# A linear-attention block rebuilt: joint query and key products, swapped halves, one reciprocal for two tiles

## The chip, the core and the metric

One core of a Trainium2 chip runs one program. TensorE (PE, with PEld for its loads of stationary operands), VectorE (DVE), ScalarE (ACT), GpSimd (POOL) and SyncE (SP, which here only issues transfers and waits) each work through their own list of instructions, and semaphores tie the lists together. The time is that of one execution on the device in microseconds; lower is better.

## What is computed

The input is 2 images of 512 channels and 32 x 32 pixels, in float32. Four layers follow each other: an attention with sampled keys and a position bias that a small network computes, a deformable convolution with a gate, a linear attention, and a multi-head attention. The change is in the third:

```python
def delu(x):
    return PARAM * jax.nn.relu(x) + jnp.exp(PARAM * jnp.minimum(x, 0.0))
xf = x.reshape(B, C, N)
Q = jnp.einsum('dc,bcn->bdn', wq, xf) + bq[None, :, None]
K = jnp.einsum('dc,bcn->bdn', wk, xf) + bk[None, :, None]
V = jnp.einsum('ec,bcn->ben', wv, xf) + bv[None, :, None]
Qf = delu(Q).transpose(0, 2, 1)
Kf = delu(K)
KV = jnp.einsum('bmn,bcn->bmc', Kf, V)
norm = 1.0 / jnp.einsum('bnd,bd->bn', Qf, jnp.sum(Kf, axis=-1) + EPS)
attn = jnp.einsum('bnd,bdc,bn->bcn', Qf, KV, norm)
return x + gamma[0] * attn.reshape(B, C, H, W)
```

B is 2, C is 512, N is 1024 pixels of an image, queries and keys have d = 64 rows and PARAM is 10.

## The kernel before

`layer2` (lines 1624 to 1858) is one block of the program: all engines enter it together and leave it together, and the next block's work begins when the last of them is done. The tile X holds the activations of both images in SBUF, 128 partitions by 4 channel groups (k) by 2048 pixels. The pixels are cut into four tiles of 512 (n; tiles 0 and 1 are image b = 0, tiles 2 and 3 image b = 1), and an image into 8 pieces of 128 pixels (c). Everything is float32.

Ahead, SP loads the query, key and value weights and the bias rows of keys and values, all counted on one semaphore `w_in`, and then the weights of the next layer (`g["prefetch"]`). TensorE, ScalarE and VectorE all wait for the five loads together.

For each image TensorE then does the following, written out at lines 1749 to 1761:

- `keys` (L1696): for each piece of 128 pixels four products, with the pixels as the stationary operand and 64 columns of key weights streamed past. So keys come out with pixels on the partitions.
- `queries` (L1687): for a tile of 512 pixels four products with 64 columns of query weights as the stationary operand. Queries come out with their 64 rows on 64 partitions.
- `pixels` (L1705): 32 transposes of X, four for each piece, in two PSUM buffers which ScalarE (L1796) and VectorE (L1838) empty in turn.
- `key_products` (L1717, L1719): keys times pixels, 8 products of 512 columns, and the sums of the keys, 8 products of one column.
- `key_values` (L1725, L1729): that result is copied, turned and multiplied by the value weights.
- `outputs` (L1738, L1746): for each tile the norms, and then four products for the four channel groups, in two PSUM buffers that VectorE adds to X (L1822).

The value weights are applied after keys and pixels have been multiplied, so values are never computed for each pixel. The features (`delu`) are made from a minimum (VectorE), an Exp (ScalarE), a maximum times ten (VectorE for keys, GpSimd for queries at L1769) and an addition (VectorE). The outputs of the first image stand behind the second image's queries, and ahead of its key products. VectorE makes the norms' reciprocals one tile after the other (L1814), each followed by a scaling of the queries (L1817):

```python
for n in range(2 * b, 2 * b + 2):
    v.wait_ge(n_mm, n + 1)
    v.reciprocal(RN[:, n, :], norms[n % 2]).then_inc(rn_ready, 1)
    v.wait_ge(rn_ready, n + 1)
    v.wait_ge(q_ready, n + 1)
    v.tensor_tensor(QN[:, n, :], QR[:, n, :], RN[:, n, :], ALU.mult).then_inc(qn_ready, 1)
```

In passing the block splits the next layer's weights into twelve rounded pieces and their remainders: ScalarE rounds (L1807), GpSimd subtracts (L1773). The block after this one begins with statistics of X on VectorE (L1969).

In the profile the tiles of this block have names with `lin_` in front, X is `net_x`.

## Time and profile before

| | |
|---|---|
| time, median of 3 runs | 4188.23 us (4186.56 to 4192.63) |
| the profiled execution's own time | 4190.17 us |
| its span | 4188.4 us |
| TensorE's mean granted clock | 0.957 of full speed |
| busy, TensorE products | 3866.5 us (92%) |
| busy, VectorE | 2981.1 us (71%) |
| busy, ScalarE | 2591.7 us (62%) |
| busy, GpSimd | 2088.0 us (50%) |

Start times in the rows below are microseconds from the start of the span. A float32 product of TensorE has two rows in the profile, each with half of the passes; a transpose has one. So "x8" is four products or eight transposes.
### The profile page before, as it was taken

Reading aid. Unit: us, or ns where it says so; the run is one execution under the profiler, and the core shown is the slowest. Engines: PE = TensorE matmul, PEld = TensorE weight load, DVE = VectorE, ACT = ScalarE, POOL = GpSimd, SP = SyncE. Lnnn points to the kernel's source line nnn. Section 1 sums busy time; section 2 is a strip of 40 time slices with the busy share of each in tenths; the row PEclk is TensorE's granted clock in tenths of the full one; section 3 lists DMA queues with packets and bytes.
Section 4 is the critical chain, followed back from the end, with each engine's and each line's share of the span. In section 5 each row is a group of like instructions: output and inputs, shape, how many; then the busy total and the mean of one; then the engine's idle time right before and its main releaser. Section 6 shows DMA issues by size and latency. Waiting matters only on the chain. (4 is left out here: it accounts for less than half of the span.)

```text
span 4188.4 us, 67038 instructions
## 1 busy us (share of the span) xinstructions
PE 3866.5 (92%) x18696; PEld 2423.2 (58%) x18696; DVE 2981.1 (71%) x4504; ACT 2591.7 (62%) x4616; POOL 2088.0 (50%) x1870
## 2 busy tenths in 40 slices
PE   6899999999999999999998999989888467969999
PEld 3555555555555555555556788837667343835553
DVE  7888888888888888888887433376999936245552
ACT  5899999999999999999996433232221431213331
POOL 0555555555555555555552455415777620036663
PEclk8999999999999999999999999999999777979999
DMA  1200000000000000000002000028999911453312
GB/s 49 103 9 12 9 10 9 9 9 9 12 9 10 9 9 9 9 12 9 10 9 87 28 5 1 0 82 340 394 390 397 377 64 62 174 116 71 72 41 81
DMA packets 150518, 326.82 MB, mean 78 GB/s; under 512 B 45785, under 2 KB 50073, under 8 KB 149517
## 3 DMA queue, kind: packets, MB, share of 16 engines
q1 hardware_dynamic: 108940, 174.46, 13.5%
q0 software_dynamic: 41472, 151.01, 9.0%
q8 instruction: 59, 0.97, 0.1%
q14 instruction: 47, 0.38, 0.0%
HBM read 246.14 MB, written 79.04 MB: 78 GB/s over the span
## 5 line engine op out<-in xcount | busy, mean ns | idle before, releaser
L558 POOL TENSOR_TENSOR cpb_sum<-cpb_tab 128x512 f32<-128x512 f32 x1028 | 1046.7, 1051 | 965.0 <-DVE cpb_r L688 964.7
L669 ACT ACTIVATE cpb_h<-cpb_z,net_vec 128x512 f32<-128x512 f32 x1536 | 1007.8, 699 | 50.5 <-PE cpb_z L609 37.8
L606 PE MATMUL cpb_z<-cpb_r,cpb_w2a 128*128 128x512 f32 x2048 | 858.1, 419 | 22.9 <-DVE cpb_h L729 22.9
L688 DVE SCALAR_TENSOR_TENSOR cpb_r<-cpb_sum,cpb_r 128x512 fp32r<-128x512 f32 x1024 | 696.7, 711 | 187.9 <-ACT cpb_r L663 187.9
L607 PE MATMUL cpb_z<-cpb_r,cpb_w2b 128*128 128x512 f32 x2048 | 802.3, 392 | 0.0
L609 PE MATMUL cpb_z<-cpb_r,cpb_w2a 128*128 128x512 f32 x2048 | 800.2, 391 | 0.0
L688 DVE SCALAR_TENSOR_TENSOR cpb_r<-cpb_z,cpb_r 128x512 fp32r<-128x512 f32 x1028 | 662.0, 686 | 160.0 <-ACT cpb_r L663 154.6
L663 ACT ACTIVATE cpb_r<-cpb_z 128x512 fp32r<-128x512 f32 x1028 | 561.1, 604 | 126.6 <-PE cpb_z L593 126.6
L663 ACT ACTIVATE cpb_r<-cpb_sum 128x512 fp32r<-128x512 f32 x1024 | 598.0, 648 | 2.0 <-POOL cpb_sum L558 2.0
L606 PEld LDWEIGHTS cpb_z<-cpb_r,cpb_w2a 128*128 128x128 f32 x2048 | 383.8, 187 | 366.1 <-issue 300.4
L618 PE MATMUL cpb_zo<-cpb_h,cpb_w3w 128*32 128x512 f32 x3584 | 477.3, 605 | 0.0
L1569 DVE SCALAR_TENSOR_TENSOR dc_acc<-dc_g,dc_wt,dc_acc 128x512 f32<-128x512 f32 x560 | 443.3, 801 | 34.9 <-DMA dc_g<-conv_out,dc_idx 19.2
L609 PEld LDWEIGHTS cpb_z<-cpb_r,cpb_w2a 128*128 128x128 f32 x2048 | 384.9, 188 | 87.4
L607 PEld LDWEIGHTS cpb_z<-cpb_r,cpb_w2b 128*128 128x128 f32 x2048 | 385.7, 188 | 63.7
L1260 POOL DMA_INDIRECT dc_g<-conv_out,dc_idx x288 | 322.9, 1121 | 169.2 <-DVE dc_acc L1569 84.8
L729 DVE TENSOR_SCALAR cpb_h<-cpb_z,net_vec 128x512 f32<-128x512 f32 x512 | 380.4, 743 | 0.0
L1442 ACT COPY dc_ys<-dc_py 128x512 f32<-128x512 f32 x144 | 84.6, 588 | 364.3 <-DMA conv_out<-dc_ys 219.2
L2262 ACT ACTIVATE net_x<-sa_pb 128x512 f32<-128x512 f32 x256 | 139.2, 595 | 267.5 <-PE sa_pb L2188 267.5
L1042 POOL TENSOR_TENSOR mlp_wb<-l_w,mlp_wa 128x512 fp32r<-128x512 f32 x128 | 196.8, 1557 | 173.5 <-ACT mlp_wa L1006 173.5
L2158 POOL TENSOR_TENSOR sa_acc<-sa_acc,net_x 128x512 f32<-128x512 f32 x192 | 240.9, 1279 | 71.5 <-ACT net_x L2262 70.6
L1326 PE MATMUL dc_py<-net_conv_w,dc_dh 128*128 128x512 f32 x576 | 234.1, 406 | 45.3 <-ACT dc_ys L1442 41.3
L2277 DVE TENSOR_REDUCE sa_mxp<-sa_pa 128x1 f32<-128x512 f32 x224 | 144.4, 686 | 147.5 <-PE sa_pa L2172 147.5
(358 smaller groups left out, 5326.5 us busy)
## 6 DMA issues: line engine op xcount, KB each, us to landing
conv_out<-dc_ys SPq DMA_DIRECT2D x576, 64.0 KB, 6.1
cpb_log<-log_dram SPq DMA_DIRECT2D x66, 256.0 KB, 3.2
qk_parts<-gn_r SPq DMA_DIRECT2D x64, 256.0 KB, 2.0
dc_wr<-in_dc_wT SPq DMA_DIRECT2D x9, 1024.0 KB, 5.9
bias_dram<-cpb_bst SPq DMA_DIRECT2D x520, 8.0 KB
net_x<-in_x SPq DMA_DIRECT2D x8, 1024.0 KB, 11.1
sa_qa<-qk_parts SPq DMA_DIRECT2D x16, 512.0 KB
sa_ka<-qk_parts SPq DMA_DIRECT2D x16, 512.0 KB
```

The source lines that it names most:

```text
L558: pool.tensor_tensor(SUM[:, r, :].rearrange("p (y x) -> p y x", x=W), TAB[:, slot, r, 0, :].unsqueeze(1).broadcast_to([P, NF // W, W]), TA ...
L606: pe.matmul(z2[:, bank, :], W2A[:], R1[:, k, :], start=True, stop=False)
L607: pe.matmul(z2[:, bank, :], W2B[:], R1[:, k, :], start=False, stop=False)
L609: pe.matmul(z2[:, bank, :], W2A[:], R2[:, k, :], start=False, stop=True).then_inc(z2_ready, 1)
L618: mm = pe.matmul(zo[32 * r:32 * r + 32, :], W3W[:, half * 4 + c, :], H2[:, (quad * 4 + r) % 8, :], start=(quad == 0), stop=False)
L663: act.activation(R1[:, t % RING, :], first_layer(t), ACT.Relu).then_inc(r1_ready, 1)
L669: act.activation(H2[:, t % 8, :], z2[:, t % 3, :], ACT.Relu, bias=V("cpb_b2")).then_inc(h2a, 1)
L688: v.scalar_tensor_tensor(R2[:, t % RING, :], first_layer(t), 0.0, R1[:, t % RING, :].bitcast(F32), ALU.max, ALU.subtract).then_inc(r2_read ...
L729: v.tensor_scalar(H2[:, (t + 2) % 8, :], z2[:, (t + 2) % 3, :], V("cpb_b2"), 0.0, ALU.add, ALU.max).then_inc(h2v, 1)
L1260: pool.indirect_dma_start(out=G[:, u % GR, y, :], out_offset=None, in_=table[tap % SLOTS][b], in_offset=bass.IndirectOffsetOnAxis(ap=IDX[: ...
L1569: v.scalar_tensor_tensor(o, G[:, u % GR, k // 2, (k % 2) * C:(k % 2 + 1) * C], WT[:, k, col:col + 1], DCB[:] if tap == 0 and k == 0 else o ...
L2158: pool.tensor_tensor(acc, ET[:, 0, u, :] if k == 1 else acc, ET[:, k, u, :], ALU.add).then_inc(added, 1)
```

## The change

The change is inside the linear attention, and in how its weights are laid out in memory. What it does:

- One weight tile `WQK` holds, for each channel group, two stationary operands of 128 columns: queries then keys for even tiles of 512 pixels, keys then queries for odd tiles. `queries_keys(n)` makes both with four products. In even tiles queries are on partitions 0 to 63 and keys on 64 to 127, in odd tiles the other way round. The products of pixels with key weights go away.
- The features of a whole tile, queries and keys, are made together: VectorE adds the bias and takes the minimum (`low`), ScalarE takes Relu of the biased product (`high`) and Exp, VectorE multiplies by ten and adds (`feature`). GpSimd has no part in it.
- Keys are turned by TensorE: 4 transposes per tile (`keys`), copied to SBUF by ScalarE, and doubled by a copy on VectorE, so that key products, sums, and all that follows from them stand on 128 partitions, twice the same 64.
- The norms of the two tiles of an image go to the two halves of one PSUM tile, on partitions 0 to 63 and 64 to 127, and VectorE takes one reciprocal of 128 partitions (`inverse`) and then scales the two tiles (`scaled`).
- The outputs read the half of the doubled operand that lies on the partitions of their queries.
- TensorE waits at its start for the joint weights only. Value weights and value biases have a semaphore of their own, waited for ahead of `key_values(0)`.
- The order of all four lists is written out by hand. The second image's keys and key products come before the outputs of the first, of which two come before the second norms and six after the second value product.

```diff
-            sp.dma_start(WQ[:], d["wqT"].rearrange("(k p) o -> p k o", p=P)).then_inc(w_in, 16)
-            sp.dma_start(WK[:], d["wkT"].rearrange("(k p) o -> p k o", p=P)).then_inc(w_in, 16)
+            sp.dma_start(WQK[:], d["wqkT"].rearrange("(k p) a o -> p k a o", p=P)).then_inc(wqk_in, 16)
             sp.dma_start(WV[:], d["wvT"].rearrange("(k p) o -> p k o", p=P)).then_inc(w_in, 16)
-            sp.dma_start(BK[:], d["bk_rows"]).then_inc(w_in, 16)
             sp.dma_start(BV[:], d["bv_rows"]).then_inc(w_in, 16)
...
-            def queries(n):
-                if n:
-                    pe.wait_ge(q_raw, n)
+            def queries_keys(n):
+                if n >= 2:
+                    pe.wait_ge(hi_ready, n - 1)
                 for k in range(CT):
-                    mm = pe.matmul(pq[:], WQ[:, k, :], X[:, k, n * NF:(n + 1) * NF], start=(k == 0), stop=(k == CT - 1))
-                mm.then_inc(q_mm, 1)
-
-            def keys(b):
-                if b:
-                    pe.wait_ge(k_raw, b)
-                for c in range(NC):
-                    at = b * HW + c * P
-                    for k in range(CT):
-                        mm = pe.matmul(pk[:, c, :], X[:, k, at:at + P], WK[:, k, :], start=(k == 0), stop=(k == CT - 1))
-                mm.then_inc(k_mm, 1)
+                    mm = pe.matmul(pq[:, n % 2, :], WQK[:, k, n % 2, :], X[:, k, n * NF:(n + 1) * NF],
+                                   start=(k == 0), stop=(k == CT - 1))
+                mm.then_inc(qk_mm, 1)
...
+            def keys(b):
+                if b:
+                    pe.wait_ge(kr_a, 2 * b)
+                    pe.wait_ge(ks_ready, b)
+                for n in range(2 * b, 2 * b + 2):
+                    pe.wait_ge(f_ready, n + 1)
+                    for c in range(NC // 2):
+                        mm = pe.transpose(pk[:, n % 2, c, :], F[:, n, c * P:(c + 1) * P], ident[:])
+                mm.then_inc(k_mm, 1)
+
...
                     pe.wait_ge(kv_ready, b)
-                    pe.wait_ge(ks_ready, b)
                 for c in range(NC):
-                    pe.matmul(pkx[:], KR[:, b, c, :], XT[:, b, c, :], start=(c == 0), stop=(c == NC - 1))
+                    pe.matmul(pks, KR[:, c].rearrange("p a d -> p (a d)"), ONE[:], start=(c == 0), stop=(c == NC - 1))
                 for c in range(NC):
-                    mm = pe.matmul(pks[:, 0:1], KR[:, b, c, :], ONE[:], start=(c == 0), stop=(c == NC - 1))
+                    mm = pe.matmul(pkx[:], KR[:, c].rearrange("p a d -> p (a d)"), XT[:, b, c, :],
+                                   start=(c == 0), stop=(c == NC - 1))
                 mm.then_inc(kx_mm, 1)
...
-            def outputs(b):
+            def norms(b):
                 pe.wait_ge(ksb_ready, b + 1)
+                if b:
+                    pe.wait_ge(rn_ready, b)
                 for n in range(2 * b, 2 * b + 2):
-                    pe.wait_ge(q_ready, n + 1)
-                    if n >= 2:
-                        pe.wait_ge(rn_ready, n - 1)
-                    pe.matmul(norms[n % 2], KSB[:, b, :], QR[:, n, :], start=True, stop=True).then_inc(n_mm, 1)
+                    rows = of_queries(n)
+                    mm = pe.matmul(pn[rows, :], KSB[rows, b, :], F[rows, n, :], start=True, stop=True)
+                mm.then_inc(n_mm, 1)
...
-            pe.wait_ge(w_in, 80)
+            pe.wait_ge(wqk_in, 16)
+            queries_keys(0)
+            queries_keys(1)
+            pixels(0)
+            queries_keys(2)
+            keys(0)
+            queries_keys(3)
             pe.wait_ge(one, 1)
-            for b in range(B):
-                keys(b)
-                queries(2 * b)
-                pixels(b)
-                queries(2 * b + 1)
-                if b:
-                    pe.wait_ge(q_raw, 2 * b + 2)
-                    outputs(b - 1)
-                key_products(b)
-                key_values(b)
-            outputs(B - 1)
+            key_products(0)
+            pixels(1)
+            pe.wait_ge(w_in, 32)
+            key_values(0)
+            norms(0)
+            keys(1)
+            key_products(1)
+            outputs(0, 0, 2)
+            norms(1)
+            key_values(1)
+            outputs(0, 2, 2 * CT)
+            outputs(1, 0, 2 * CT)
...
-            for n in range(NT):
-                pool.wait_ge(q_raw, n + 1)
-                pool.tensor_scalar(QR[:, n, :], QT[:, n, :], 0.0, PARAM, ALU.max, ALU.mult).then_inc(q_high, 1)
-                if n == 1:
-                    for i, (whole, high, low) in enumerate(PIECES):
...
+            high(0)
+            exponential(0)
+            high(1)
+            pixels(0, 0)
+            exponential(1)
+            for c in range(2, NC, 2):
+                pixels(0, c)
+            high(2)
+            keys(0)
+            exponential(2)
+            high(3)
+            exponential(3)
+            act.wait_ge(weights_in, 64)
+            for i, (whole, part, _) in enumerate(PIECES):
+                act.copy(part, whole).then_inc(split_h, 1)
+            for c in range(0, NC, 2):
+                pixels(1, c)
+            key_products(0)
+            keys(1)
+            key_products(1)
...
+            def low(n):
+                v.wait_ge(qk_mm, n + 1)
+                v.tensor_scalar(LO[:, n, :], pq[:, n % 2, :], V("bqk", n % 2), 0.0, ALU.add, ALU.min).then_inc(lo_min, 1)
+
+            def feature(n):
+                v.wait_ge(hi_ready, n + 1)
+                v.wait_ge(lo_exp, n + 1)
+                v.scalar_tensor_tensor(F[:, n, :], HI[:, n, :], PARAM, LO[:, n, :], ALU.mult, ALU.add).then_inc(f_ready, 1)
...
+            def keys(b):
+                v.wait_ge(kr_a, 2 * b + 2)
+                v.tensor_copy(KR[:, :, 1, :], KR[:, :, 0, :]).then_inc(kr_v, 1)
...
+            def inverse(b):
+                v.wait_ge(n_mm, b + 1)
+                if b:
+                    v.wait_ge(qn_ready, 2 * b)
+                v.reciprocal(RN[:], pn[:]).then_inc(rn_ready, 1)
+
+            def scaled(n):
+                rows = of_queries(n)
+                v.wait_ge(rn_ready, n // 2 + 1)
+                v.tensor_tensor(QN[rows, n // 2, :], F[rows, n, :], RN[rows, :], ALU.mult).then_inc(qn_ready, 1)
...
+            low(0)
+            low(1)
+            feature(0)
+            pixels(0, 1)
+            feature(1)
+            for c in range(3, NC, 2):
+                pixels(0, c)
+            low(2)
+            keys(0)
+            feature(2)
+            low(3)
+            feature(3)
+            key_sums(0)
+            for c in range(1, NC, 2):
+                pixels(1, c)
+            v.wait_ge(w_in, 32)
+            key_values(0)
+            inverse(0)
+            keys(1)
+            scaled(0)
+            scaled(1)
+            key_sums(1)
+            output(0)
+            output(1)
+            inverse(1)
+            scaled(2)
+            scaled(3)
+            key_values(1)
+            for i in range(2, NT * CT):
+                output(i)
...
-            "wqT": i["L2_wq"].T, "wkT": i["L2_wk"].T, "wvT": i["L2_wv"].T,
-            "bk_rows": every(i["L2_bk"]), "bv_rows": every(i["L2_bv"])[0:DH],
+            "wqkT": np.stack([np.concatenate([i["L2_wq"], i["L2_wk"]]).T, np.concatenate([i["L2_wk"], i["L2_wq"]]).T], axis=1),
+            "wvT": i["L2_wv"].T, "bv_rows": every(i["L2_bv"]),```

TensorE's list of the block, first its beginning to the first value product, before. `pk` holds keys, `pq` queries, `px` what is transposed, `pkx` key products and values, `pks` the sums:

```order
L1696 MATMUL lin_pk<-lin_wk,net_x 128x64 x32
L1687 MATMUL lin_pq<-net_x,lin_wq 64x512 x4
L1705 MATMUL lin_px<-net_ident,net_x 128x128 x32
L1687 MATMUL lin_pq<-net_x,lin_wq 64x512 x4
L1717 MATMUL lin_pkx<-lin_xt,lin_kr 64x512 x8
L1719 MATMUL lin_pks<-lin_one,lin_kr 64x1 x8
L1725 MATMUL lin_px<-net_ident,lin_kx 128x64 x4
L1729 MATMUL lin_pkx<-lin_wv,lin_kxt 64x512 x4
```

And the same place on TensorE in the changed program, where `pk` holds the turned keys and the sums:

```order
L1688 MATMUL lin_pq<-net_x,lin_wqk 128x512 x8
L1698 MATMUL lin_px<-net_ident,net_x 128x128 x32
L1688 MATMUL lin_pq<-net_x,lin_wqk 128x512 x4
L1709 MATMUL lin_pk<-net_ident,lin_f 128x128 x8
L1688 MATMUL lin_pq<-net_x,lin_wqk 128x512 x4
L1719 MATMUL lin_pk<-lin_one,lin_kr 128x1 x8
L1721 MATMUL lin_pkx<-lin_xt,lin_kr 128x512 x8
L1698 MATMUL lin_px<-net_ident,net_x 128x128 x32
L1732 MATMUL lin_px<-net_ident,lin_kx 128x128 x4
L1736 MATMUL lin_pkx<-lin_wv,lin_kxt 128x512 x4
```

The 32 products of 64 columns ahead of the first queries are gone; the queries and keys of both images and the second image's transposes have moved ahead of the first value product.

TensorE's list from the first norms to the end of the block, before (`pq` and `pk` take the norms, `pa` the outputs):

```order
L1738 MATMUL lin_pq<-lin_qr,lin_ksb 64x512
L1738 MATMUL lin_pk<-lin_qr,lin_ksb 64x512
L1746 MATMUL lin_pa<-lin_qm,lin_kv 128x512 x8
L1717 MATMUL lin_pkx<-lin_xt,lin_kr 64x512 x8
L1719 MATMUL lin_pks<-lin_one,lin_kr 64x1 x8
L1725 MATMUL lin_px<-net_ident,lin_kx 128x64 x4
L1729 MATMUL lin_pkx<-lin_wv,lin_kxt 64x512 x4
L1738 MATMUL lin_pq<-lin_qr,lin_ksb 64x512
L1738 MATMUL lin_pk<-lin_qr,lin_ksb 64x512
L1746 MATMUL lin_pa<-lin_qm,lin_kv 128x512 x8
```

And in the changed program, where `pn` takes the norms of both tiles and `pq` the outputs:

```order
L1745 MATMUL lin_pn<-lin_f,lin_ksb 64x512 x2
L1709 MATMUL lin_pk<-net_ident,lin_f 128x128 x8
L1719 MATMUL lin_pk<-lin_one,lin_kr 128x1 x8
L1721 MATMUL lin_pkx<-lin_xt,lin_kr 128x512 x8
L1756 MATMUL lin_pq<-lin_qn,lin_kv 128x512 x2
L1745 MATMUL lin_pn<-lin_f,lin_ksb 64x512 x2
L1732 MATMUL lin_px<-net_ident,lin_kx 128x128 x4
L1736 MATMUL lin_pkx<-lin_wv,lin_kxt 128x512 x4
L1756 MATMUL lin_pq<-lin_qn,lin_kv 128x512 x14
```

The outputs of the first image have moved behind the key products of the second, and 14 of 16 now stand in one row at the end.

VectorE's list in the changed program, from the first value result to the second:

```order
L1865 SCALAR_TENSOR_TENSOR lin_kv<-lin_bv,lin_ks,lin_pkx 128x512
L1871 RECIPROCAL lin_rn<-lin_pn 128x512
L1855 COPY lin_kr<-lin_kr 128x8x64
L1876 TENSOR_TENSOR lin_qn<-lin_f,lin_rn 64x512 x2
L1859 COPY lin_ks<-lin_pk 128x1
L1861 TENSOR_SCALAR lin_ksb<-lin_ks 128x64
L1882 SCALAR_TENSOR_TENSOR net_x<-lin_pq,net_vec,net_x 128x512 x2
L1871 RECIPROCAL lin_rn<-lin_pn 128x512
L1876 TENSOR_TENSOR lin_qn<-lin_f,lin_rn 64x512 x2
L1865 SCALAR_TENSOR_TENSOR lin_kv<-lin_bv,lin_ks,lin_pkx 128x512
```

Each reciprocal is one of 128 partitions, and the copy that doubles the second image's keys stands behind the first of them.

## Rows read from the trace of the kernel before

**Rows 1.** Timeline of the transfer queue: start us, us, what; its first load.

```profile
3384.45 0.41 SPq L1670 DMA_DIRECT2D lin_wq<-in_wqT  x1
```

**Rows 2.** Timeline of VectorE, the block's last addition.

```profile
3514.01 0.75 DVE L1822 SCALAR_TENSOR_TENSOR net_x<-lin_pa,net_vec,net_x 128x512 f32<-128x512 f32 x1 [0.96 <-PE lin_pa L1746]
```

**Rows 3.** Timeline of TensorE's products: start us, us, what, count, idle time before.

```profile
3393.39 13.92 PE L1696 MATMUL lin_pk<-lin_wk,net_x 128*128 128x64 f32 x64 [13.56 <-DMA lin_bv<-in_bv_rows]
3407.23 5.89 PE L1687 MATMUL lin_pq<-net_x,lin_wq 128*64 128x512 f32 x8
3413.06 1.10 PE L1705 MATMUL lin_px<-net_ident,net_x 128*128 128x128 f32 x8
3414.39 4.08 PE L1705 MATMUL lin_px<-net_ident,net_x 128*128 128x128 f32 x24 [0.24 <-ACT lin_xt L1796]
3418.40 3.65 PE L1687 MATMUL lin_pq<-net_x,lin_wq 128*64 128x512 f32 x8
...
3428.75 1.04 PE L1719 MATMUL lin_pks<-lin_one,lin_kr 128*64 128x1 f32 x16
3430.46 0.46 PE L1725 MATMUL lin_px<-net_ident,lin_kx 64*128 64x64 f32 x4 [0.67 <-ACT lin_kx L1799]
3431.38 5.34 PE L1729 MATMUL lin_pkx<-lin_wv,lin_kxt 128*64 128x512 f32 x8 [0.46 <-ACT lin_kxt L1801]
3436.66 7.36 PE L1696 MATMUL lin_pk<-lin_wk,net_x 128*128 128x64 f32 x64
...
3457.29 1.07 PE L1738 MATMUL lin_pq<-lin_qr,lin_ksb 64*64 64x512 f32 x2 [0.77 <-ACT lin_qt L1783]
3458.20 1.02 PE L1738 MATMUL lin_pk<-lin_qr,lin_ksb 64*64 64x512 f32 x2
3462.61 3.75 PE L1746 MATMUL lin_pa<-lin_qm,lin_kv 64*128 64x512 f32 x4 [3.39 <-DVE lin_qm L1817]
3467.16 10.60 PE L1746 MATMUL lin_pa<-lin_qm,lin_kv 64*128 64x512 f32 x12 [0.81 <-DVE net_x L1822]
...
3488.39 3.65 PE L1729 MATMUL lin_pkx<-lin_wv,lin_kxt 128*64 128x512 f32 x8 [0.46 <-ACT lin_kxt L1801]
```

**Rows 4.** Busy us by stretch: PE, PEld, DVE, ACT, POOL; then PEclk, DMA share, GB/s.

```profile
3411.00:3414.00 3.00, 3.00 (x12) 1.23 (x10) 0.00 (x0) 0.84 (x2) 0.07 (x1) 0.87 0.00 0
...
3417.00:3420.00 3.00, 2.87 (x13) 1.44 (x13) 1.71 (x3) 0.59 (x2) 0.00 (x0) 1.00 0.00 0
...
3432.00:3435.00 3.00, 3.00 (x6) 0.81 (x4) 0.00 (x0) 3.00 (x7) 2.04 (x2) 0.54 0.01 3
...
3441.00:3444.00 3.00, 3.00 (x28) 2.93 (x28) 0.00 (x0) 0.00 (x0) 3.00 (x4) 1.00 0.00 0
...
3459.00:3462.00 3.00, 0.21 (x1) 0.00 (x0) 2.96 (x2) 0.00 (x0) 0.46 (x1) 0.60 0.00 0
...
3474.00:3477.00 3.00, 3.00 (x5) 0.95 (x3) 1.50 (x2) 0.00 (x0) 0.00 (x0) 0.50 0.00 0
```

**Rows 5.** Loads of the block: queue, operation, count, KB, median us from issue to landing.

```profile
l3o_w_qk<-in_w_qkT SPq DMA_DIRECT2D x1, 2048.0 KB, 12.4
lin_wv<-in_wvT SPq DMA_DIRECT2D x1, 1024.0 KB, 5.5
...
lin_wq<-in_wqT SPq DMA_DIRECT2D x1, 128.0 KB, 2.4
```

**Rows 6.** Groups of instructions by form, block alone: busy us, mean ns, idle before.

```profile
L1822 DVE SCALAR_TENSOR_TENSOR net_x<-lin_pa,net_vec,net_x 128x512 f32<-128x512 f32 x16 | 11.8, 746 | 12.6 <-PE lin_pa L1746 12.6
L1773 POOL TENSOR_TENSOR l3w_wq_low<-l3o_w_qk,l3w_wq_high 128x512 fp32r<-128x512 f32 x8 | 11.1, 1420 | 0.0
...
L1814 DVE RECIPROCAL lin_rn<-lin_pq 64x512 f32<-64x512 f32 x2 | 6.7, 3350 | 1.3 <-PE lin_pq L1738 1.3
...
L1779 ACT ACT_TABLE_LOAD x1 | 1.3, 1283 | 27.8 <-DVE lin_km L1831 27.8
...
L1831 DVE TENSOR_SCALAR lin_km<-lin_kt 128x512 f32<-128x512 f32 x2 | 0.9, 438 | 0.1
```

More of the change, by code:

```diff
@@ new lines, in exponential, with pixels @@
+            def exponential(n):
+                act.activation(LO[:, n, :], LO[:, n, :], ACT.Exp, scale=PARAM).then_inc(lo_exp, 1)
+            def pixels(b, c):
+                act.wait_ge(xt_mm, b * NC + c + 1)
+                act.copy(XT[:, b, c, :], px[:, 0, :]).then_inc(xt_a, 1)
+            def keys(b):
+                act.wait_ge(k_mm, b + 1)
+                if b:
+                    act.wait_ge(kx_mm, b)
+                for n in range(2):
+                    act.copy(KR[:, n * NC // 2:(n + 1) * NC // 2, 0, :], pk[:, n, :, of_keys(n)]).then_inc(kr_a, 1)
```

171 lines of the change are left out of this document (65 added, 106 removed).

## The prediction

> **What bounds the kernel now.** The change touches one block of the program, the linear attention. The page's shares are averages over all blocks and say nothing of it, so I read its stretch in the timelines of the queue and of VectorE for the ends, in TensorE's timeline for the order, then in the table of stretches with the granted clock, and last in the lists of loads and of groups by form for prices.
>
> The block begins with its loads at 3384.45 [rows 1] and ends with VectorE's last addition at 3514.01 plus 0.75, so 3514.76 [rows 2]: 130.3 us. TensorE's rows [rows 3], in which every float32 product counts twice and a transpose once, are to be read as one chain: apart from two waits they follow each other almost without a gap, so TensorE bounds the block, and its waits are at the start (13.56 us until the last of five loads, the rows of value biases, has landed) and in the middle (3.39 us until VectorE has finished the reciprocals). The reader is to see three more things in these rows. The 32 key products of 64 columns cost 13.92 us the first time and 7.36 us the second. The outputs cost 10.60 us for six products, 1.71 each once the tail of about 0.3 is taken off, where the query products cost 3.65 for four, 0.91 each. The value product costs 5.34 once and 3.65 the other time. Each of these is a factor of up to two, and the clock column explains all of them [rows 4]: 0.50 is 1.2 GHz and 1.00 is 2.4 GHz. It is 0.50 during the outputs, 1.00 in the second key stage, 0.54 in the stretch of the slow value product. It fell at the reciprocals (0.60 in 3459 to 3462). At the first query product (3407.23) it was low and a mean of 0.87 over 3411 to 3414 puts its rise 0.26 of the way in, at 3411.8, 4.5 us after that product began. The key stage before it had kept TensorE busy for 13.9 us without a rise.
>
> **The change part by part.** I rebuild TensorE's chain, since it orders everything. Durations are those of one profiled execution of 4190.17 us, 1.9 above the median of the runs.
>
> *Start.* TensorE now waits for one load, the joint weights of 512 KB. Nearest rows: 128 KB lands 2.4 us after its issue, 1024 KB behind others after 5.5 [rows 5]. So it lands between 3386.9 and 3390.0; I take 3.1 us, 3387.6, nearer the small one because nothing is queued ahead of it. TensorE starts there instead of at 3393.39: 5.8 us earlier (3.4 to 6.5).
>
> *Queries and keys.* 64 key products in two stages (13.92 + 7.36) and 16 query products of 64 columns become 16 products of 128 columns. The output of 128 columns costs no more time if the cost goes by the 512 streamed columns: 0.91 at 2.4 GHz. The first two groups start at 1.2 GHz: 4.5 us at 1.71 each give 2.6 products, the other 5.4 at 0.91 give 4.9, together **9.4 us**. Groups 2 and 3 are 3.65 each. The keys now have to be turned by 16 transposes, 0.1375 each from 8 in 1.10 [rows 3]: 1.1 per half. Together 3.65 + 1.1 + 3.65 = **8.4**.
>
> *Pixels.* The 32 transposes of a half stay; they are paced by the copies, 0.68 per four (24 in 4.08 [rows 3]), 5.4 per half. In the first half the two copying engines now also make the first features, and ScalarE loads its Exp table (1283 ns [rows 6]) between the first query result and the second. On VectorE the features of tile 1 wait for ScalarE's second Exp ahead of its second copy, which puts the last transposes 0.4 later: **5.8 and 5.4**.
>
> *Key products.* The 8 products of 512 columns per half stay, 8 x 0.91 = 7.3. The sums move ahead of them and their stationary operand is now 128 columns wide: 16 loads of 64 columns took 1.04, 64 loads of 128 columns 7.36, 0.115 each, so 16 take 1.85. **9.15 per half**, twice.
>
> *Values.* First half: wait for ScalarE's copy 0.6, transposes 0.55, wait for the next copy 0.65 (it was 0.46 for a tile half as wide, and 0.67 was the wait for the first copy [rows 3]), product 3.65: **5.45**. Second half: the first copy lies under the norms, so 0.55 + 0.6 + 3.65 = 4.8.
>
> *Norms and reciprocals.* The four norm products stay, 0.9 each, the pitch from 3457.29 to 3458.20 [rows 3]. Per half, two reciprocals of 64 partitions (3350 ns each [rows 6]) become one of 128 partitions; no row has one of 128, and bounds are 3.35, if the 512 elements of a partition set it, and 6.7, if all elements do. I take 3.35, since the operations on 128 partitions beside it have 512 elements too and take 0.44 and 0.75 [rows 6], no more per element of a partition than its own. In the first half it stands ahead of the copy that doubles the keys (0.44 from the nearest operation with one input between SBUF tiles [rows 6]) on VectorE, and the key products of the second half are queued behind that copy: norms **1.8**, then **3.9** until TensorE goes on, under which the 8 transposes of keys (1.1) are hidden. In the second half it is covered by the value product, 0.55 + 0.6 + 3.65 = 4.8 against 3.35 + 1.3 for the two scalings; nothing waits. If that cover went, 3.35 would return.
>
> *Outputs.* Two of the first half's outputs go before the second norms (1.8, and norms 1.8, values 4.8: together **8.4**), and 14 stand at the end. VectorE needs 746 ns for one [rows 6], below TensorE's 0.91; with two buffers I take 0.95 each, **13.3**, if the clock is at 2.4 GHz, and the last addition 0.75.
>
> Sum: 9.4 + 5.8 + 8.4 + 9.15 + 5.4 + 5.45 + 1.8 + 3.9 + 9.15 + 8.4 + 13.3 + 0.75 = 80.9, so the end at 3468.5, 46.3 us earlier.
>
> *The clock gives some back.* The wait of 3.9 follows two 64-row products; in the trace such a wait brought 1.2 GHz (0.60 in 3459 to 3462 [rows 4]). The sums and the first products after it then run slow: the sums at 13.92/64 = 0.2175 a load instead of 0.115, 1.7 more, and some 3.4 us of products at half rate, 1.7 more: 3.4. Before each value product stand transposes and two short waits; there the clock fell in one of two cases, at 5.34 - 3.65 = 1.7: 1.7 for the two. 46.3 - 5.1 = **41.2 us**.
>
> *At nothing.* ScalarE's twelve rounding copies of the next layer's weights now stand ahead of its second set of pixel copies; they end about when the first key products do. GpSimd loses its four feature operations and keeps twelve subtractions at 1420 ns [rows 6], 17 us from about 3414, done before VectorE's next copy between SBUF tiles on the path; if that copy met them it could cost 1 us. SP's loads for the next layer stand behind a first load that is 256 KB bigger; the longest took 12.4 us from its issue [rows 5], and its first use moves to about 3413, 28 us after the block's start. Everything after the block reads what it read before and only starts earlier.
>
> Where the two norm products of a half stand in the array is new: they now use different halves of its rows and of its columns. The rows have products of this shape one behind the other, at a pitch of 0.9 [rows 3], and the sum takes them so; side by side they would cost 0.9 a half less. The Trainium skill, "TensorE: Matmul & The Clock Gate", Part 3 (Packing small matmuls), says that products in different row groups run concurrently; by it the sum would be 79.1 in place of 80.9. No row here shows such a pair, so this stands as rival E.
>
> **The rivals.**
>
> *A, the forecast: the last 14 outputs run at 2.4 GHz.* For it: at the second key stage TensorE's work was light too (short streams between loads), and a clock that was high stayed high (1.00 in 3441 to 3444), though the same stage had not raised a low one; and a pixel stage kept it as well (1.00 in 3417 to 3420) [rows 4]. The outputs come directly behind the value product, not behind an idle wait. 41.2 us off.
>
> *B: the outputs run at 1.2 GHz.* For it: the output stage of the trace did, for 10.6 us of unbroken work (0.50 in 3474 to 3477 [rows 4]); and half of the array's rows are idle in them. 14 x (1.71 - 0.95) = 10.6 comes back: 30.6 us off.
>
> *C, slower: the clock never rises in the block.* Place: the first two groups of query-key products. Price: 60 products of 512 columns at 1.71 (102.6), sums 7.0, 64 pixel transposes at twice 0.1375 (17.6), 24 others 6.6, waits 5.4 and the last addition 0.75 give 140, and the end at 3527.6, 12.8 us later than before. Between 46.3 us faster with the clock always high from its rise on and 12.8 slower without a rise, 8.4 slower is passed when (46.3 + 8.4)/(46.3 + 12.8) = 93% of the work lies at the low clock. Against it: the same kind of product raised the clock after 4.5 us.
>
> *D: a queue of VectorE or ScalarE becomes the bound.* Each now holds work of two stages in one fixed order. If the wide reciprocal costs 6.7, 3.35 is added in the middle and 3.2 at the end; with lost overlap at the first features (2 us) 33 us are left. That is another size and no other sign.
>
> *E: as A, with the two norm products of a half side by side.* 0.9 less per half: 43.0 us off. Against it: every float32 product in the rows waits for the one before it. For it speaks only the new placement, and beside it the rule of the Trainium skill named above.
>
> **How the numbers follow.** A 0.50, E 0.10, B 0.32, D 0.05, C 0.03. The time is A's: 4188.23 - 41.2 = 4147.0. The range reaches down to no clock loss at all with paired norms (46.3, or 4142, less 1.8 for the norms and 1 for the spread of runs) and up to B with a late load and a slower start (30.6 - 2.4 - 1 = 27, 4161): 4139 to 4161. A's own range is 4139 to 4152. A change of 0.2% (8.4 us) is about what can be told from none: faster 0.96; same 0.02, from part of C and unforeseen waits; slower 0.02, C.
>
> **What would show it.** In the new profile: TensorE's first product near 3387.6 after the block's start; the clock reaching 1.00 about 4.5 us later; a wait of TensorE of about 2.8 behind the first 128-partition reciprocal with that reciprocal at 3.35; GpSimd's first work in the block being the subtractions; outputs at a pitch of 0.95 (A) or 1.71 (B); the block's length near 89 us against 130.3. The prediction is wrong if the pitch of the 128-column products at the high clock isn't 0.91, if the reciprocal grows with its partitions, or if the clock falls in stages that I took as kept.

## The result and the profile after

The changed kernel takes 4144.35 us (median of 4 runs, 4142.98 to 4146.59), the kernel before 4189.68 us in the same comparison (4 runs). The ratio is 0.9892, 95% interval 0.988 to 0.9904: 45.3 us faster. Forecast were 4147.0 us and 41.2 us off.

The profiled execution took 4143.60 us, with a span of 4141.8. The whole program is not a sharp measure of this change: the blocks ahead of it vary by some microseconds from one execution to the next. So I read the block itself, from the issue of its first load to the end of its last addition. It took 130.3 us before [rows 1, 2]. The first fence is the transfer queue's timeline of the changed kernel at both ends of the block (the second row opens the next block), the second the last row of VectorE in the block.

```profile
3381.66 0.40 SPq L1672 DMA_DIRECT2D lin_wqk<-in_wqkT  x1
...
3467.94 0.34 SPq L1948 DMA_DIRECT2D layer_input<-net_x  x1
```

```profile
3466.05 1.61 DVE L1882 SCALAR_TENSOR_TENSOR net_x<-lin_pq,net_vec,net_x 128x512 f32<-128x512 f32 x2 [0.42 <-PE lin_pq L1756]
```

3467.66 - 3381.66 = 86.0 us: 44.3 less. The rest of the difference of the two spans (46.6) lies ahead of the block, which began 2.8 us earlier, and behind it, 0.5 the other way; nothing was changed there.

TensorE's timeline of the changed kernel (start us, us, what, idle before), whose rows answer to [rows 3]:

```profile
3385.91 8.60 PE L1688 MATMUL lin_pq<-net_x,lin_wqk 128*128 128x512 f32 x16 [8.82 <-DMA lin_wqk<-in_wqkT]
3394.34 1.04 PE L1698 MATMUL lin_px<-net_ident,net_x 128*128 128x128 f32 x8
3396.55 1.09 PE L1698 MATMUL lin_px<-net_ident,net_x 128*128 128x128 f32 x8 [1.17 <-ACT lin_xt L1798]
...
3400.41 3.60 PE L1688 MATMUL lin_pq<-net_x,lin_wqk 128*128 128x512 f32 x8
...
3408.16 1.84 PE L1719 MATMUL lin_pk<-lin_one,lin_kr 128*128 128x1 f32 x16
3409.86 7.11 PE L1721 MATMUL lin_pkx<-lin_xt,lin_kr 128*128 128x512 f32 x16
3416.81 1.04 PE L1698 MATMUL lin_px<-net_ident,net_x 128*128 128x128 f32 x8
...
3422.89 0.63 PE L1732 MATMUL lin_px<-net_ident,lin_kx 128*128 128x128 f32 x4 [0.21 <-issue]
3424.19 3.70 PE L1736 MATMUL lin_pkx<-lin_wv,lin_kxt 128*128 128x512 f32 x8 [0.68 <-ACT lin_kxt L1815]
3427.82 1.08 PE L1745 MATMUL lin_pn<-lin_f,lin_ksb 64*64 64x512 f32 x4
3428.83 1.09 PE L1709 MATMUL lin_pk<-net_ident,lin_f 128*128 128x128 f32 x8
3432.64 3.03 PE L1719 MATMUL lin_pk<-lin_one,lin_kr 128*128 128x1 f32 x16 [2.72 <-DVE lin_kr L1855]
3435.53 9.37 PE L1721 MATMUL lin_pkx<-lin_xt,lin_kr 128*128 128x512 f32 x16
3444.83 1.98 PE L1756 MATMUL lin_pq<-lin_qn,lin_kv 64*128 64x512 f32 x4
3446.74 1.08 PE L1745 MATMUL lin_pn<-lin_f,lin_ksb 64*64 64x512 f32 x4
3447.75 0.66 PE L1732 MATMUL lin_px<-net_ident,lin_kx 128*128 128x128 f32 x4
...
3452.71 14.15 PE L1756 MATMUL lin_pq<-lin_qn,lin_kv 64*128 64x512 f32 x28
```

And the clock. Columns are busy us of PE, PEld, DVE, ACT and POOL, then the granted clock, the DMA share and GB/s, of the changed kernel:

```profile
3387.00:3390.00 3.00, 3.00 (x6) 1.30 (x5) 0.00 (x0) 0.00 (x0) 0.00 (x0) 0.68 1.06 380
...
3417.00:3420.00 3.00, 2.36 (x20) 1.89 (x18) 2.20 (x4) 1.17 (x2) 3.00 (x4) 1.00 0.00 0
3420.00:3423.00 3.00, 2.10 (x16) 1.42 (x14) 1.50 (x3) 1.66 (x3) 3.00 (x3) 1.00 0.00 0
...
3432.00:3435.00 3.00, 2.36 (x14) 2.36 (x14) 1.86 (x4) 0.00 (x0) 0.00 (x0) 0.71 0.00 0
3435.00:3438.00 3.00, 3.00 (x7) 1.68 (x7) 0.00 (x0) 0.00 (x0) 0.00 (x0) 0.50 0.00 0
...
3462.00:3465.00 3.00, 2.85 (x7) 0.71 (x6) 2.37 (x4) 0.00 (x0) 0.00 (x0) 1.00 0.00 0
```

The reader is to see one long wait in the middle (2.72 us, for VectorE's doubling copy behind the reciprocal), one stretch at 1.2 GHz in the work behind it, and the last 14 outputs at 2.4 GHz, where the outputs before ran at 1.2 (0.50 in [rows 4]). The clock did not fall during the wait: a mean of 0.71 over 3432 to 3435 puts the fall near 3433.3, 0.6 us after the sums had begun. It had risen at about 3388.9 (0.68 over 3387 to 3390), 3.0 us after the first product, where the prediction took 4.5.

The same block in groups, in us of TensorE's timeline from the first row of a group to the first of the next:

| | before | after | difference |
|---|---|---|---|
| first issue to first product | 8.9 | 4.3 | -4.7 |
| queries and keys, and after also the first image's turned keys | 38.4 | 16.2 | -22.2 |
| pixel transposes | 10.7 | 12.2 | +1.5 |
| sums and key products (before, with the wait for ScalarE's copy behind them) | 18.4 | 20.8 | +2.5 |
| value products and their transposes | 12.2 | 9.9 | -2.4 |
| norms, reciprocals, outputs to the end; after, also the second image's turned keys and the wait of 2.72 | 41.6 | 22.7 | -19.0 |
| block | 130.3 | 86.0 | -44.3 |

Half of the gain is in the queries and keys, where the joint product is, and most of the other half in the outputs and what they waited for.

### The profile page after: what moved, and what is told of

It is laid out like the page before. It is cut to its first block and busy times, and to the rows that moved or that the text cites. A ratio compares the mean times of both kernels' runs of the same rounds, so it can differ in the third digit from the quotient of the medians.

```text
span 4141.8 us, 66808 instructions
## 1 busy us (share of the span) xinstructions
PE 3829.4 (92%) x18584; PEld 2402.4 (58%) x18584; DVE 2973.9 (72%) x4496; ACT 2592.3 (63%) x4618; POOL 2081.1 (50%) x1866
## 6 DMA issues: line engine op xcount, KB each, us to landing
dc_wr<-in_dc_wT SPq DMA_DIRECT2D x9, 1024.0 KB
net_x<-in_x SPq DMA_DIRECT2D x8, 1024.0 KB, 8.7
```

## The experiments

Block lengths below are measured as above, from each run's own trace. Whole times of single executions stand beside them only for completeness.

**Start: wait for all loads.**

```diff
             pe.wait_ge(wqk_in, 16)
+            pe.wait_ge(w_in, 32)
             queries_keys(0)
```

> The changed kernel, TensorE's first product waiting for the value weights and value biases too. The changed kernel's block (first load to last addition) takes 86.0 us, its first product begins 4.25 us after the first load's issue, and the last of the three loads lands 6.6 us after an issue at 1.0, so at 7.6. Theory (TensorE's chain sets the block, and the start is a term of it): block 86.0 + 3.3 = 89.3 us. Rival (the start is absorbed by a later wait for VectorE or by the clock rising at a fixed time): under 1 us longer.

Block 88.6 us (4145.5 us in all). TensorE's first row:

```profile
3389.46 9.42 PE L1688 MATMUL lin_pq<-net_x,lin_wqk 128*128 128x512 f32 x16 [11.53 <-DMA lin_bv<-in_bv_rows]
```

The start came 3.4 us later than in the changed kernel (7.7 after the first issue against 4.3), where 3.3 was expected, and the first eight products took 0.8 longer. But 1.7 came back: the stretch at the low clock behind the long wait was shorter here (sums and products end 10.5 us after the wait, against 12.2). So the start is a plain term of the chain, and the clock's part in a stage differs between executions by up to 1.7 us even where the program there is the same. That limits what a single run can say.

**Two reciprocals of 64 partitions instead of one of 128.**

```diff
-                v.reciprocal(RN[:], pn[:]).then_inc(rn_ready, 1)
+                v.reciprocal(RN[0:D], pn[0:D]).then_inc(rn_part, 1)
+                v.reciprocal(RN[D:P], pn[D:P]).then_inc(rn_ready, 1)
...
```

(TensorE's second norms and VectorE's scalings wait for `rn_part` too.)

> The changed kernel with two reciprocals of 64 partitions in place of each one of 128. Theory (a reciprocal costs by the elements of a partition, 3.35 us whatever the partitions, and stands on the path in both halves): 3.4 us longer wait of TensorE ahead of the second half's sums, and some 3 us later outputs at the end, because only about 0.2 us of VectorE's second reciprocal is uncovered now; block 86.0 + 6.5 = 92.5 us. Rival (the second is covered by the value product): 86.0 + 3.4 = 89.4 us.

Block 101.9 us (4163.1 in all): 15.9 longer, against 6.5 and 3.4. VectorE's two reciprocals, and TensorE's rows at the two places, in this run:

```profile
3433.85 3.35 DVE L1873 RECIPROCAL lin_rn<-lin_pn 64x512 f32<-64x512 f32 x1 [0.19 <-PE lin_pn L1747]
3437.23 3.36 DVE L1874 RECIPROCAL lin_rn<-lin_pn 64x512 f32<-64x512 f32 x1
```

```profile
3441.10 3.58 PE L1720 MATMUL lin_pk<-lin_one,lin_kr 128*128 128x1 f32 x16 [6.28 <-DVE lin_kr L1857]
...
3461.93 1.98 PE L1758 MATMUL lin_pq<-lin_qn,lin_kv 64*128 64x512 f32 x4
3466.85 19.95 PE L1758 MATMUL lin_pq<-lin_qn,lin_kv 64*128 64x512 f32 x24 [2.94 <-DVE net_x L1886]
```

```profile
3474.00:3477.00 3.00, 3.00 (x6) 0.99 (x4) 1.50 (x2) 0.00 (x0) 0.00 (x0) 0.50 0.00 0
```

The reciprocal costs 3.36 us for 64 as for 128 partitions, so the joint one saves exactly one each time. The first half paid what was expected (a wait of 6.28 for 2.72). The surprise is the second: its 3.4 us made TensorE wait 2.94 us between its outputs, and after that wait the outputs ran at 1.2 GHz to the end, 25.7 us from the value product to the end of the block against 15.0. The theory had the right place and missed what follows from it. This is what rival B forecast of the outputs, brought about by one reciprocal: in the changed kernel nothing idles in front of the last outputs, and they are at 2.4 GHz. Of the rest, 0.8 is in the sums and key products, which ran at the low clock for longer, and 0.9 at the block's start (first products 1.1 longer, load 0.2 sooner), which the edit doesn't touch.

**Outputs of the first image ahead of the key products of the second.**

```diff
-            key_products(1)
-            outputs(0, 0, 2)
+            outputs(0, 0, 2 * CT)
+            key_products(1)
             norms(1)
             key_values(1)
-            outputs(0, 2, 2 * CT)
             outputs(1, 0, 2 * CT)
```

(VectorE's list follows it.)

> The changed kernel with all eight outputs of the first image ahead of the second image's key products, as in the kernel before. Same work, other order. Theory (the place of the outputs behind a wait for the reciprocal makes them run at 1.2 GHz): eight outputs at a pitch of 1.71 in place of 1.01, 5.6 us, and a wait 1.3 us longer, since outputs need the scaled queries: block 86.0 + 7 = 93 us, granted clock 0.50 in these outputs. Rival (the order is worth nothing, the outputs are only moved): within 1.5 us of 86.0, clock 1.00 in them.

Block 94.4 us (4152.7 in all): 8.4 longer, expected 7.

```profile
3434.74 12.72 PE L1756 MATMUL lin_pq<-lin_qn,lin_kv 64*128 64x512 f32 x16 [3.39 <-DVE lin_qn L1875]
...
3467.89 8.07 PE L1756 MATMUL lin_pq<-lin_qn,lin_kv 64*128 64x512 f32 x16 [0.84 <-DVE lin_kv L1864]
```

```profile
3436.00:3439.00 3.00, 3.00 (x4) 0.98 (x4) 1.49 (x2) 0.00 (x0) 0.00 (x0) 0.50 0.00 0
```

Eight outputs take 12.7 us behind a wait of 3.39, and the other eight 8.1 behind the value product. Of the 8.4 us, 4.7 are in the outputs, 1.4 in the sums and key products behind the first eight, 0.7 in the longer wait, 0.9 in the new wait ahead of the last eight, and 0.7 at the block's start (first products 0.9 longer, load 0.2 sooner), which the edit doesn't touch. More than half of what the order is worth is the clock's.

**Norm products kept apart.**

```diff
-                    mm = pe.matmul(pn[rows, :], KSB[rows, b, :], F[rows, n, :], start=True, stop=True)
-                mm.then_inc(n_mm, 1)
+                    pe.matmul(pn[rows, :], KSB[rows, b, :], F[rows, n, :], start=True, stop=True).then_inc(n_mm, 1)
+                    if n % 2 == 0:
+                        pe.wait_ge(n_mm, n + 1)
...
```

(VectorE's reciprocal then waits for both.)

> The changed kernel with TensorE waiting for the first norm product of a half before it issues the second. Four rows took 1.08 us in the changed kernel. Theory (the two products ran side by side and both halves' norms are on the path): 1.0 us longer per half, block 88.0 us. Rival (norm rows are short for another reason, such as missing records, or are covered): under 0.5 us longer.

Block 90.7 us (4151.6 in all).

```profile
3431.55 2.20 PE L1745 MATMUL lin_pn<-lin_f,lin_ksb 64*64 64x512 f32 x4
...
3451.58 2.20 PE L1745 MATMUL lin_pn<-lin_f,lin_ksb 64*64 64x512 f32 x4
...
3455.03 5.40 PE L1736 MATMUL lin_pkx<-lin_wv,lin_kxt 128*128 128x512 f32 x8 [0.67 <-ACT lin_kxt L1816]
```

Two products take 2.20 us apart and 1.08 together: they did run side by side. That is 2.2 of the 4.7 us, 1.1 a half. Not all of it is the pairing's: two norm products at the pitch of 0.9 in [rows 3] would take 1.8 a half, 0.8 more than the pair's 1.0, so some 0.3 a half, an estimate, is the semaphore wait that the edit adds. Another 1.7 is the value product behind the second pair, which met the low clock here (5.40 against 3.70), and 0.8 is at the block's start (first products 1.0 longer, load 0.3 sooner), which has nothing to do with the edit. Whether the longer norms brought the low clock, one run can't tell.

**The doubling copy ahead of the reciprocal.**

```diff
-            inverse(0)
             keys(1)
+            inverse(0)
             scaled(0)
```

> The changed kernel with VectorE's copy that doubles the second image's keys ahead of the first reciprocal. TensorE's wait of 2.72 us ahead of the sums ends with ScalarE's copy and this one, at about 1.2 us. Theory (the loss in the second half's key products is the clock's, brought by the long wait): clock stays at 1.00, sums 1.84 and products 7.1 in place of 3.03 and 9.37: 1.5 + 3.4 = 4.9 us shorter, block 81.1 us. Rival (the clock falls because of the light work around the wait, norms and transposes, whatever the wait's length): 1.5 us shorter only, 84.5 us.

Block 81.9 us (4141.6 in all), 4.1 shorter.

```profile
3434.75 1.95 PE L1719 MATMUL lin_pk<-lin_one,lin_kr 128*128 128x1 f32 x16 [1.20 <-DVE lin_kr L1855]
3436.56 7.11 PE L1721 MATMUL lin_pkx<-lin_xt,lin_kr 128*128 128x512 f32 x16
```

The wait fell by 1.5 and the sums and key products by 3.3; the first eight products took 1.1 more than in the changed kernel and the load landed 0.3 sooner. In this run the clock stayed up, as the theory had it.

**Three unread products in the wait**, which leaves the wait's end where it was and adds work whose result nothing reads.

```diff
             keys(1)
+            for k in range(3):
+                pe.matmul(pq[:, 0, :], WQK[:, k, 0, :], X[:, k, 0:NF], start=True, stop=True)
             key_products(1)
```

> The changed kernel with three products more of 512 columns, whose result nobody reads, in TensorE's wait ahead of the second half's sums; they take about 2.6 of its 2.72 us. Theory (idle time brings the low clock): clock 1.00 through the sums and products, 3.4 us shorter, block 82.6 us, with the wait for VectorE otherwise as before. Rival (the clock's fall has another cause, as the norm products of 64 rows): no change, 86.0, or up to 0.3 longer.

Block 82.4 us, 3.6 shorter. The whole execution took 4154.9, because the block only began at 3396.52 there: a good case of why the block is read and not the total.

```profile
3444.34 2.74 PE L1774 MATMUL lin_pq<-net_x,lin_wqk 128*128 128x512 f32 x6
3447.22 1.95 PE L1719 MATMUL lin_pk<-lin_one,lin_kr 128*128 128x1 f32 x16
3449.02 7.11 PE L1721 MATMUL lin_pkx<-lin_xt,lin_kr 128*128 128x512 f32 x16
```

```profile
3447.00:3450.00 3.00, 2.86 (x20) 2.31 (x20) 1.44 (x3) 0.00 (x0) 0.00 (x0) 1.00 0.00 0
```

The sums begin 3.81 us after the key transposes do, exactly as in the changed kernel, and are then followed by products at full speed. In this run work without use, put where TensorE had been idle, was worth 3.3 us, as the theory had it. Two things limit it. It is one execution. And in the runs with the wait of 2.72 us the clock fell 0.6 to 1.6 us after the sums had begun and not in the wait, so the sums, norms and transposes around the wait may have a part in it; no run separates them from the wait.

**Outputs in pairs.** One output of the even tile and one of the odd stand next to each other in TensorE's list, and four PSUM buffers take them (the two of `px` are free by then).

```diff
-                    n, m = divmod(i, CT)
+                    n, m = place(i)
...
+        def place(i):
+            return i // (2 * CT) * 2 + i % 2, i % (2 * CT) // 2
+
+        def buffer(i):
+            return pa[:, i % 2, :] if i // 2 % 2 == 0 else px[:, i % 2, :]
...
```

> The changed kernel with outputs in pairs, one of the even tile and one of the odd, whose operands lie on different halves of the partitions, and four PSUM buffers for them in place of two. In the changed kernel 14 outputs take 14.15 us, 1.01 each, against 0.80 per addition on VectorE and about 0.86 per product. Theory 1 (products on different halves of the rows run side by side, as the norms): VectorE becomes the bound, 14 x 0.80 = 11.3, block 3 us shorter, 83 us, and TensorE idle between pairs. Theory 2 (they do not, as both write all columns; the two buffers were the limit): TensorE at 0.87 each, 12.2, block 84 us, TensorE without gaps.

Block 79.9 us (4138.2 in all), 6.1 shorter, TensorE and VectorE at the end of the block:

```profile
3443.82 1.13 PE L1764 MATMUL lin_pq<-lin_qn,lin_kv 64*128 64x512 f32 x4
...
3450.85 1.13 PE L1764 MATMUL lin_px<-lin_qn,lin_kv 64*128 64x512 f32 x4
```

```profile
3458.61 1.40 DVE L1890 SCALAR_TENSOR_TENSOR net_x<-lin_pq,net_vec,net_x 128x512 f32<-128x512 f32 x2
3459.92 1.40 DVE L1890 SCALAR_TENSOR_TENSOR net_x<-lin_px,net_vec,net_x 128x512 f32<-128x512 f32 x2
```

Two outputs take 1.13 us against 1.98, so theory 1 holds, and VectorE is the bound, back to back. It is even quicker than expected: a pair of additions starts every 1.32 us, against 2.03 in the changed kernel (pairs at 3464.02 and 3466.05 there), where VectorE waited 0.42 for TensorE ahead of each pair and a pair took 1.61 and not 1.40. The order and the number of buffers changed together here, so what four buffers would give in the old order is not shown. From the value product to the block's end it is 10.5 us against 15.0. The first pair gave 0.9, and 1.7 is a shorter stretch at the low clock behind the long wait, against 0.9 lost at the block's start.

**Both together.**

> Doubling copy first and paired outputs together. If both gains hold and are independent: 86.0 - 4.9 - 3 = 78 us for the block, some 4136 us in all. If the outputs' gain is lost, because VectorE is behind at their start: 81 us.

Block 77.2 us, 4133.7 in all. It was then timed:

> The kernel of the run with doubling copy first and paired outputs, timed. Its one execution took 4133.7 us. If the block's 77.5 us there are its usual length, 53 us below the kernel before: 4136 (4132 to 4140), and 8 us below the changed kernel. If that one execution was a lucky phase of the clock: 4140 to 4144.

(The block of that one execution was 77.2 us.)

4133.88 us (median of 4 runs, 4132.33 to 4137.55) against 4187.15 for the kernel before; ratio 0.987, interval 0.9854 to 0.9886. The changed kernel, in its own comparison, stood at 0.9892 (0.988 to 0.9904), and its four runs all lie above these four. Block 77.5 us. In this profile the key products met the low clock all the same, behind a wait of 1.20 us:

```profile
3434.55 8.81 PE L1727 MATMUL lin_pkx<-lin_xt,lin_kr 128*128 128x512 f32 x16
```

```profile
3435.00:3438.00 3.00, 3.00 (x5) 1.20 (x4) 2.32 (x3) 0.00 (x0) 0.00 (x0) 0.54 0.00 0
```

So the shorter wait doesn't keep the clock for certain, and the fall comes later still: in this trace near 3435.2, 2.5 us after the sums had begun. Over all runs whose sums and key products stand behind the wait of 2.72 us, these took 10.5 to 12.2 us, where 8.85 is the price at the high clock: 1.7 to 3.3 lost, four times of four. Behind 1.20 us they lost 1.7 in two executions of four.

**Pixel copies ahead of the second tile's features**, on ScalarE and VectorE, on top of both.

```diff
             exponential(0)
-            high(1)
             pixels(0, 0)
+            high(1)
             exponential(1)
```

> The same, and in the first tiles both copying engines empty the pixel buffers ahead of the second tile's features. TensorE waits 1.17 us there now, for ScalarE's copy behind its second Relu. Theory (ScalarE's order is that wait): the wait falls to about 0.3, block 0.8 us shorter, which the runs' spread of some 3 us hides but the trace shows. Rival (the wait only moves to a later transposition, since features are made later on the same engines): block unchanged within 0.3 us, apart from the clock's phase.

4134.09 us (4130.12 to 4136.35), ratio 0.9869 (0.9852 to 0.9885): no difference to the kernel above. Block 76.9 us. The wait did fall:

```profile
3395.55 1.20 PE L1704 MATMUL lin_px<-net_ident,net_x 128*128 128x128 f32 x8 [0.24 <-ACT lin_xt L1806]
3397.14 0.66 PE L1704 MATMUL lin_px<-net_ident,net_x 128*128 128x128 f32 x4 [0.38 <-ACT lin_xt L1806]
3398.06 1.09 PE L1704 MATMUL lin_px<-net_ident,net_x 128*128 128x128 f32 x8 [0.27 <-DVE lin_xt L1859]
```

But the stage went only from 6.1 to 5.7 us, since the later groups of transposes wait a little more. Most of the wait moved, as the rival had it.

**Two parts tried on the kernel before.** First, queries ahead of keys:

```diff
-                keys(b)
                 queries(2 * b)
+                keys(b)
                 pixels(b)
```

> The kernel before with TensorE making the first tile's queries of an image ahead of its keys, nothing else. Its block takes 130.3 us. Theory (the first key stage took 13.92 us, not 7.36, only because short streams do not raise the clock, and the queries do): queries 5.9, keys 7.4: 6.5 us shorter, block 124 us. Rival (the key stage is slow at the start because of the loads running beside it until 3402): no more than 1 us shorter.

Block 128.3 us, only 2.0 shorter, and yet the mechanism is the expected one:

```profile
3388.15 5.66 PE L1687 MATMUL lin_pq<-net_x,lin_wq 128*64 128x512 f32 x8 [12.31 <-DMA lin_bv<-in_bv_rows]
3393.74 7.36 PE L1696 MATMUL lin_pk<-lin_wk,net_x 128*128 128x64 f32 x64
...
3405.45 4.94 PE L1705 MATMUL lin_px<-net_ident,net_x 128*128 128x128 f32 x24 [3.47 <-ACT lin_xt L1796]
```

The key stage fell from 13.92 to 7.36 us with the clock at 1.00. It was given back in a new wait of 3.47 us (and one of 2.81 in the second half): ScalarE makes the keys' Exp ahead of its pixel copies, and with the keys later the transposes are what waits. The edit removed time at the low clock and uncovered a queue: 6.6 us less in the keys, 6.5 more in the two pixel stages. The 2.0 us that are left lie elsewhere, for the most part: the first value product met the high clock (3.65 against 5.34) and the load landed 0.5 sooner, against 0.9 more in the second half's key products.

Second, TensorE waiting at the start for query and key weights alone:

```diff
-            pe.wait_ge(w_in, 80)
+            pe.wait_ge(qk_in, 32)
             pe.wait_ge(one, 1)
```

The other loads are waited for at their first use.

> The kernel before with TensorE starting when query and key weights have landed, and the value weights, value and key biases waited for where they are used. The first product came 8.94 us after the first load's issue. Theory (start is a plain term of TensorE's chain): query and key weights land about 3 us after the first issue; 5.9 us shorter, block 124.4 us. Rival (as in the changed kernel the loads behind it slow the first ones, landing at 4.25): 4.7 us shorter, 125.6.

```profile
3385.78 13.91 PE L1698 MATMUL lin_pk<-lin_wk,net_x 128*128 128x64 f32 x64 [6.79 <-DMA lin_wk<-in_wkT]
```

Block 126.1 us, 4.2 shorter. The start itself came 6.0 sooner, 2.9 us after the first issue; stretches at the low clock took 1.8 back (the second half's products 9.47 against 8.23, its value product 5.20 against 3.65, the first queries 4.92 against 5.89). With the value weights behind the small loads here too, the 4.3 us after which the changed kernel starts are most likely its bigger first load's own.

## Why the prediction was right, step by step

The time (4144.4 against 4147.0) and case A were right, and case E (0.10) came with it: the outputs at 2.4 GHz and the norm products side by side. That the number came out so near is in part luck. For the block the forecast was 89.1 us (130.3 - 41.2) against 86.0, and its terms are off both ways: those that came out longer than forecast add 3.0 us, those that came out shorter 6.1. By the terms of the sum:

| term | predicted | measured |
|---|---|---|
| first issue to first product | 3.15 | 4.25 |
| first two groups of queries and keys | 9.4 | 8.4 |
| pixels, first and second half | 5.8, 5.4 | 6.1, 6.1 |
| two more groups and turned keys | 8.4 | 7.75 |
| sums and key products, first half | 9.15 | 8.65 |
| values, first half | 5.45 | 4.9 |
| norms, first half | 1.8 | 1.0 |
| until TensorE goes on | 3.9 | 3.8 |
| sums and key products, second half | 9.15 + 3.4 | 12.2 |
| two outputs, norms, values | 8.4 | 7.9 |
| last outputs and last addition | 13.3 + 0.75 | 14.95 |
| clock at the value products | 1.7 | 0 |

- *Start*: mis-sized. The load of 512 KB landed 4.2 us after its issue, not 3.1, nearer the large row than I took it. A load of 128 KB in the early start on the kernel before still landed in 2.3, with the value weights behind it too.
- *Queries and keys*: right in kind. The pitch of a product is 3.44/4 = 0.86 us (3400.41 to 3403.85), not 0.91, and the prediction had named another pitch than 0.91 as a sign of being wrong; I had divided rows' durations, which carry one tail each, in place of differences of starts. The output of 128 columns costs no more than that of 64. The first groups' low clock was near, if 1.5 us shorter in this trace: 8.4 to 10.0 us in eleven traces, 9.4 forecast.
- *Pixels*: forecast 0.7 too short for the second image. VectorE's tiny operation that spreads the first image's sums (L1861) stands in that stage and took 1.28 us there, beside GpSimd's subtractions (3410.9 to 3425.8); the second image's took 0.20, without them. I had put GpSimd's load on the copy only and priced it at nothing. That GpSimd is the cause is read from these rows and not tested, and so is its part in the 0.7. VectorE's timeline of the changed kernel:

```profile
3417.21 1.28 DVE L1861 TENSOR_SCALAR lin_ksb<-lin_ks 128x64 f32<-128x64 f32 x1
...
3445.13 0.20 DVE L1861 TENSOR_SCALAR lin_ksb<-lin_ks 128x64 f32<-128x64 f32 x1
```

- *Norms*: I kept the serial price because no row had such a pair. The row 1.08 for two, and 2.20 with a wait between them, decide for rival E. By the rule named there from the Trainium skill, "TensorE: Matmul & The Clock Gate", Part 3 (Packing small matmuls), the pair costs about one product; the trace agrees, for float32 too and for outputs (1.13 a pair).
- *Reciprocal*: right, 3.36 us on 128 partitions and on 64, so case D's 6.7 did not come.
- *The wait and the clock behind it*: right in place and size, 3.8 us, and 12.2 against 8.85 at the high clock. The other runs with the same wait lost 1.7 or 3.3, so that this execution met the 3.4 taken is chance. The run with unread products agrees with the wait as the cause, in one execution; what of it is the wait's and what the work's around it stays open.
- *Clock at the value products*: 1.7 was too much for this kernel, where it was at 1.00; it did happen in the run with norms apart and in the early start on the kernel before. The Trainium skill says in Part 4 (PE-mode transpose) of the same page that the full clock does not engage for transposes. Here the clock was already high and stayed at 1.00 through 6 us of transposes with waits between (3417 to 3423 above); whether transposes alone could raise it, no run shows.
- *Last outputs*: 1.01 each, not 0.95, with two buffers and one order of tiles. With four buffers and the tiles in turn they took 0.66 each, VectorE's pace; which of the two changes did it isn't separated.
- *Case B*, at 0.32, was a real danger and not a phantom: one more reciprocal brought it for the last twelve outputs (101.9 us).

Where the gain came from was measured by undoing one part, in one execution each, for the joint weights' start (3.4 us), the single reciprocal (15.9, of which 3.6 are the first wait, 10.7 the second with its clock and 0.9 not the edit's), the outputs' order (8.4, of which 0.7 not the edit's), and the paired norms (2.2 with the added wait). They overlap through the clock and don't add up. The joint product's 22 us were read from rows, not undone; the run with queries first shows that 6.6 of them were the first key stage at 1.2 GHz. What decides when the clock falls, and for how long, from one execution to the next stays open.

## What to carry to other kernels

Where TensorE bounds a stretch, ask of each wait what clock the work behind it will have: products that keep a high clock may not raise a low one (the outputs here), so their place behind dense work or behind a wait can be worth more than the wait itself. Put half-array work of two tiles on different partition halves and next to each other (the outputs that gained by it had four buffers), and give one VectorE operation all 128 partitions. And price a stage by differences of start times, not by its rows' durations.

## What the runs showed that I had not expected

- Two float32 products on different halves of the partitions run side by side: norms 1.08 us a pair (2.20 apart), outputs 1.13 (1.98 for two of the same half).
- Outputs of 64 rows kept 2.4 GHz for 14 us and, behind a wait of 2.94 us in another run, stayed at 1.2 GHz for 20 us: 14.15 us for fourteen in the one case, 19.95 for twelve in the other.
- A VectorE operation of 128 x 64 took 1.28 us while GpSimd subtracted and 0.20 when it did not.
- The clock fell 0.6 to 2.5 us after TensorE had gone on from a wait of 2.72 or 1.20 us, and not in the wait; ahead of the outputs it fell inside a wait of 2.94.
- The stretch at the low clock behind the same wait cost from 1.7 to 3.3 us in different executions, and the block's first eight products took from 8.4 to 10.0 us; so the block's length in a single run is not to be read closer than 2 to 3 us, and a difference is to be looked for stage by stage.
